# Attention stacks filled by 6 transfers of 32 rows in place of 12 transfers of 16 rows

## What is computed

```
q, k, v = heads of (normalised, modulated x) @ Wqkv + bias      # 16 heads x 16 dimensions
att     = softmax(q @ k^T * scale)                              # 512 x 512 for each head
x       = x + gate * ((att @ v) @ Wproj + bias)
x       = x + gate * (gelu(norm(x) @ W1 + b1) @ W2 + b2)        # blocks 0, 1, 2
```

## Time and profile before

| | us |
|---|---|
| median of 3 runs (lowest, highest) | 1201.08 (1197.64, 1203.54) |
| the profiled execution: its time | 1197.83 |
| its span in the profile | 1196.0 |
| TensorE matmuls busy | 1116.3 (93%) |
| TensorE weight loads busy | 713.5 (60%) |
| ScalarE busy | 806.0 (67%) |
| VectorE busy | 706.2 (59%) |
| POOL busy | 487.5 (41%) |
| DMA: bytes, mean rate | 64.49 MB, 54 GB/s |
| mean granted TensorE clock | 0.966 of full speed |

### The profile page before, as it was taken

The page is one execution under the profiler, slowest core; times in us unless marked ns, Lnnn a source line. Parts: engine busy times, 40 slices in busy tenths (PEclk is TensorE's granted clock), DMA queues, the critical chain, the costliest instruction groups (busy, mean ns, idle before and its releaser), DMA issues.

```text
span 1196.0 us, 19984 instructions
## 1 busy us (share of the span) xinstructions
PE 1116.3 (93%) x6681; PEld 713.5 (60%) x6681; DVE 706.2 (59%) x1448; ACT 806.0 (67%) x1439; POOL 487.5 (41%) x443
## 2 busy tenths in 40 slices
PE   8889999789989989999999999999999999999886
PEld 6566876654656556656556666566566466445343
DVE  7544556535264373335865855856847747888783
ACT  2563656387887688786677686687775676676563
POOL 1542642513642525453255354254353253435042
PEclk9899999899999989999999999999999999999897
DMA  7000001224414203331242232133213303342401
GB/s 227 19 26 27 1 18 22 44 52 98 87 34 82 53 15 82 65 63 20 43 89 66 57 72 45 19 77 59 56 24 54 63 1 76 55 80 44 79 14 44
DMA packets 40997, 64.49 MB, mean 54 GB/s; under 512 B 11816, under 2 KB 26920, under 8 KB 40896
## 3 DMA queue, kind: packets, MB, share of 16 engines
q1 hardware_dynamic: 40896, 63.21, 25.6%
HBM read 22.90 MB, written 2.12 MB: 21 GB/s over the span
## 4 chain that ended last, share of the span: by engine, by line
PE 64%; ACT 11%; DVE 10%; issue 8%; POOL 3%; SPq 3%; DMA 1%; ACTq 0%; POOLq 0%; DVEq 0%
PE ring L584 12%; PE ring L585 11%; PE ring L586 11%; PE AVB L694 10%; PE ring L681 8%; PE ring L658 4%; ACT probs L872 4%; DVE m L1180 3%; SPq L537 3%; PE ring L714 2%; DVE stats L1038 1%; DVE m L1164 1%; ACT L872 1%; ACT gT_h L938 1%; PE ring L627 1%
## 5 line engine op out<-in xcount | busy, mean ns | idle before, releaser
L872 ACT ACTIVATE probs<-ring 128x512 f32<-128x512 f32 x768 | 399.1, 615 | 147.2 <-PE ring L658 83.9
L1180 DVE TENSOR_REDUCE m<-ring 128x1 f32<-128x512 f32 x512 | 318.7, 682 | 126.2 <-PE ring L658 111.9
L681 PE MATMUL ring<-SQ,SK 49*128 49x512 f32 x768 | 238.0, 445 | 18.7 <-ACT probs L872 8.3
L658 PE MATMUL ring<-SK,SQ 48*128 48x512 f32 x512 | 200.0, 461 | 4.2 <-ACT probs L872 2.4
L681 PEld LDWEIGHTS ring<-SQ,SK 49*128 49x128 f32 x768 | 112.2, 189 | 153.4 <-issue 77.1
L694 PE MATMUL AVB<-probs,V 128*32 128x512 f32 x1536 | 197.1, 624 | 0.0
L1281 POOL TENSOR_TENSOR gT_l<-gT_f,gT_h 128x512 fp32r<-128x512 f32 x96 | 121.1, 1283 | 82.8 <-ACT gT_h L938 80.9
L584 PE MATMUL ring<-w_h,gT_h 128*128 128x256 f32 x384 | 110.7, 288 | 1.0 <-POOL gT_l L1281 0.7
L658 PEld LDWEIGHTS ring<-SK,SQ 48*128 48x128 f32 x512 | 86.5, 188 | 37.7 <-ACT probs L872 28.0
L585 PE MATMUL ring<-w_l,gT_h 128*128 128x256 f32 x384 | 108.0, 281 | 0.0
L586 PE MATMUL ring<-w_h,gT_l 128*128 128x256 f32 x384 | 107.8, 281 | 0.0
(11 more groups left out here) (182 smaller groups left out, 2128.7 us busy)
## 6 DMA issues: line engine op xcount, KB each, us to landing
SQ<-qh SPq DMA_DIRECT2D x192, 64.0 KB, 2.3
SK<-kh SPq DMA_DIRECT2D x192, 64.0 KB, 2.3
SQ<-ql SPq DMA_DIRECT2D x96, 64.0 KB, 2.3
SK<-kl SPq DMA_DIRECT2D x96, 64.0 KB, 2.3
raw<-in_w SPq DMA_DIRECT2D x20, 256.0 KB, 2.8
wmod_s<-in_wmod SPq DMA_DIRECT2D x6, 512.0 KB, 5.0
gates<-gate_rows SPq DMA_DIRECT2D x12, 256.0 KB, 3.6
raw<-in_wqkv SPq DMA_DIRECT2D x9, 256.0 KB, 2.8
```

The source lines that it names most:

```text
L658: mm = pe.matmul(o[:, :], SQ[a % 4][r:r + KS, n // 2, c * P:(c + 1) * P], SK[a % 4][r:r + KS, n // 2, :], start=True, stop=True)
L681: mm = pe.matmul(o[:, :], SK[a % 4][r:r + KS + 1, n // 2, c * P:(c + 1) * P], SQ[a % 4][r:r + KS + 1, n // 2, :], start=True, stop=True)
L872: act.activation(probs[:, n % PROBS, :], bank(kind, a, i)[:, :], ACT.Exp, scale=SCALE[layer(unit_job(a))]).then_inc(done["scores"], 1)
L1180: nc.vector.tensor_reduce(m16[:, 80 * (a % 2) + col:80 * (a % 2) + col + 1], bank(kind, a, i)[:, :], AX_X, ALU.max, negate=True).then_inc( ...
```

## The change

The row of dimension d, part r, of a half is now 64 * half + 4 * d + r. A part is thus the rows r, r + 4, r + 8, ... of the whole tile, and the 32 contiguous source rows of both halves fill them in one transfer of 32 partitions x 4 KB (128 KB): 6 DMAs for a unit, not 12. The order of the rows in a contraction is free, as long as SQ and SK have the same one. The rows 3, 7, ..., 63 of a half have no part. The last of them (63, KS = BLK - 1) is the shift row. The others are zero in SQ and one in SK, and add nothing. A max matmul contracts 63 rows where it had 48, a scores matmul 64 where it had 49. SQ has to be set to zero once, which four memsets on POOL do before the diagonal of ident is made. Everything else stays.

```diff
-KS = 3 * HD
+KS = BLK - 1
 ...
         def STACK_IN(u):
-            return 16 * 12 * ((u - UNITS * BATCH) // 4 + 1)
+            return 16 * 6 * ((u - UNITS * BATCH) // 4 + 1)
 ...
                     for stack, parts in ((SQ[a % 4], (qh, ql, qh)), (SK[a % 4], (kh, kh, kl))):
                         for r, part in enumerate(parts):
-                            for par in range(2):
-                                src = part[2 * HD * g + HD * par:2 * HD * g + HD * par + HD, :, :]
-                                dst = stack[BLK * par + HD * r:BLK * par + HD * r + HD, :, :]
-                                sp.dma_start(dst.bitcast(F32), src.bitcast(F32)).then_inc(stacked[a % 4], 16)
+                            src = part[2 * HD * g:2 * HD * g + 2 * HD, :, :]
+                            sp.dma_start(stack[r:P:4, :, :].bitcast(F32), src.bitcast(F32)).then_inc(stacked[a % 4], 16)
 ...
             link(nc.gpsimd.memset(ident[:, :], 0.0))
+            for i in range(4):
+                link(nc.gpsimd.memset(SQ[i][:, :, :].bitcast(F32), 0.0))
             pool.wait_ge(dve_seq, 1)
```

## The result

| | before | after |
|---|---|---|
| median, us (lowest to highest, runs) | 1199.45 (1197.64 to 1203.54, 4) | 1181.33 (1180.6 to 1182.63, 4) |
| ratio, 95% interval | | 0.9859 [0.9828, 0.9891] |
| profiled execution: time, span, mean granted clock | 1197.83, 1196.0, 0.966 | 1181.5, 1179.7, 0.979 |

The change makes the kernel 1.4% faster, 18.1 us by the medians and 16.3 us between the two profiled executions. The prediction had 5.4 us less and a range that ended at 1187. The gain is over three times the one forecast and lies outside the range.

What follows compares the result with a forecast made beforehand. The prediction took TensorE, nearly full in blocks 2 and 3, as the bound, with two shift-row waits of 4.7 us behind SP's stacks. Terms 3.65 + 1.0 + 0.25 + 0.5 = 5.4 us gave 1195.7 us, range 1187 to 1203.

Steps and rivals of the forecast that it cites:

- Matmuls: TensorE's 1280 max and scores matmuls: 63 or 64 rows take as long as 48 or 49; 0 us.
- Issue on SP: SP's stack issues halve, so shift rows go out sooner at units 55 and 59: 3.65 us less, bounds 0 to 4.7.
- The clock behind the long wait: TensorE after its 3.44 us wait at unit 59: clock may no longer fall; 1.0 us less, bounds 0 to 1.5.
- First max of a unit: TensorE's max matmul waiting for the whole stack: 0.25 us less, at unit 40 only.
- Weight loads behind a stack: ScalarE's 2.76 us idle at 659.6 us, its load queued behind unit 38's stack: 0.5 us less, bounds 0 to 2.76.
- The transfers themselves: DMA engines: same bytes, 0.73 us for a 32-row transfer against 0.36 for one of 16; the sum stays the same.
- Rival C: DMA engines: denser transfers with spread rows land later, making the kernel slower, 1205.4 us; chance 0.15.
- Start: Four POOL memsets, about 0.95 to 5.1 us, hidden in POOL's wait until 5.57: 0 us, bounds 0 to 3.8.
- Rival D: Kernel start: POOL's memsets are not covered and cost 3.8 us, giving 1199.5 us; chance 0.05.
- Sum: Whole kernel: 3.65 + 1.0 + 0.25 + 0.5 = 5.4 us less, from a median of 1201.08 to 1195.7 us.
- Rival A: SP's 30 us in the chain set the pace; halving them gives 15 us, 1186 us; chance 0.18.
- Rival B: Gain absorbed by VectorE's maxima or ScalarE's exponentials; 0 to 3 us remain, about 1199.5 us; chance 0.15.

Runs made afterwards that it cites:

- e_rows: Kernel before with its 12 transfers, but contractions of 63 and 64 rows and SQ zeroed by memsets on POOL: 1192.55 us, ratio 0.997.
- e_memset: Kernel before with only the four memsets of SQ on POOL added: 1198.69 us, ratio 1.0014.
- e_47: Kernel after, still six transfers, with contractions cut to 47 and 48 rows (last 4 of each head's 16 dimensions left out): 1188.18 us, ratio 0.9924.
- The pair at unit 60: e_35 beside a repeat of the unchanged kernel after (1183.63 us, ratio 0.9871), compared 8 us before and behind unit 60's shift transpose.
- e_split: Kernel after with each transfer cut in two: 12 transfers of 16 rows, still four apart, 63 and 64 rows contracted: 1194.95 us, ratio 0.9979.
- e_35: Kernel after, still six transfers, with contractions cut to 35 and 36 rows (7 of each head's 16 dimensions left out): 1195.26 us, ratio 0.9992.

## Why the prediction was wrong

**Matmuls.** This is the step that failed. It asked whether 15 more rows make a matmul longer, found that they don't (right: 440 and 459 ns against 445 and 461), took 0 and wrote "Below nothing: a faster one is not plausible". What the rows change is not the length of a matmul at a given clock but the clock over thousands of them. e_rows against e_memset has 18.9 us less at half clock by the rows alone, the kernel after against e_47 19.3 us less, and with the six transfers in place that is 6.0 us of time where the prediction had 0. At 0.33 us each, 19.3 us are 6.4. The row that could have raised the question stood in the text: 0.95 of full clock from 940 to 1160 us while TensorE was 94% busy. Two waits of 4.7 us could not account for it.

The two profiled executions put the clock higher than that: 83.4 - 51.2 = 32.2 us less at half clock, 10.6 us of their 16.3. The means over all executions have 22.8 us less, 7.5 of 15.1 us: the profiled execution of the kernel before had more time at half clock than most.

The Trainium skill (TensorE: Matmul & The Clock Gate, What's actually happening) says that the clock is set by how busy the array has been recently. The pair at unit 60 does not bear this out for the share of time with a matmul in flight: in the 8 us ahead that share was equal, and then the clocks were 0.57 and 1.00.

**Issue on SP.** Right in mechanism and in size at its two places: 3.6 us for 3.65, 2.69 us from copy to scores for 2.67, 0.59 us for an issue of 32 rows. Its reach was undersized. It was priced on the kernel as it stood. e_rows and e_split show that with more rows and 12 transfers the waits are 7.6 and 7.2 us, so the shorter queue is also what lets the clock's gain through. And the transfers as a whole brought 9.1 us in e_47, where the prediction's whole sum was 5.4: 3.5 us of waits, 1.1 of the weight load below and 1.2 of the clock are 5.8, and some 3 us stay unexplained.

**The clock behind the long wait.** Right where it was placed. The kernel before takes 4.24 us for eight matmuls and an av group behind the long wait; the kernel after takes 3.01 us from 1097.53 us to
```profile
1100.54 0.50 PE L680 MATMUL ring<-SQ,SK 64*128 64x512 f32 x1
```
That is 1.2 us for the 1.0 forecast. The error was to think of the clock only there.

**First max of a unit** and **Weight loads behind a stack.** 0.25 and 0.5 us. The first is too small to be told apart. For the second, TensorE's instructions after 662 us stand 1.1 us further ahead than those before it, and ScalarE's wait is gone: twice the estimate, inside its bounds. e_47 has the same lead there.

**The transfers themselves.** The sum took 0, rightly, but 0.73 us a transfer was too much. The queue's share fell from 25.6% of 1196.0 us to 20.2% of 1179.7 us, 306 to 238 us on each engine. There are 576 stack rows of 4 KB on each, so 0.12 us less for a row. The packets in the trace say the same: a packet of 4 KB took 0.38 us on average before and 0.26 after. The queue also has 4608 packets fewer (40896 and 36288), one of 4 bytes for each of the 288 transfers saved and each of the 16 engines. The Trainium skill's two figures (SBUF — State Buffer, Door 1: The DMA port swizzle), worked out per port, are 26 GB/s with 4 ports and an estimated 24 with 8, for transfers of 1 MiB, so a row would take no less time; here it takes 30% less in the larger transfer, and the measurement decides. It is the size of the transfer and not the four-apart rows: e_split, with 16 rows four apart, has 25.7%. Rival C is out by this. That 97 GB/s agreed with the skill's 104 was luck: the window's rate was set by the pace of the issues, 64 KB every 0.63 us, with the engines 0.58 busy.

**Start.** Covered, as predicted. POOL's timeline after:
```profile
0.98 3.98 POOL L1262 MEMSET SQ<- 128x1024 f32 x4
5.57 0.29 POOL L1264 TENSOR_SCALAR_AFFINE_SELECT ident<-ident 128x128 f32<-128x128 f32 x1 [0.61 <-DVE sq L958]
```
The four end at 4.96 us and the diagonal starts at 5.57 as before. VectorE's own memsets ran beside them and took 0.91 us each, as before. Rival D is out, and e_memset (1.0014) confirms it.

**Sum.** For the two profiled executions: 3.6 (waits) + 10.6 (clock) + 1.1 (weight load) = 15.3 of 16.3 us. By the means over all executions: 3.6 + 7.5 + 1.1 = 12.2 of 15.1 us, so about 3 us stay unexplained. The same sum by means gives e_rows 15.0 x 0.33 - 2.9 = 2.1 us against 3.6, e_split 11.8 x 0.33 - 2.5 = 1.4 against 2.4, e_47 5.8 against 9.1. What is missing is largest in the two kernels with six transfers. The waits and the weight load are from one profile of each. Part of the miss in absolute time is the base: 1201.08 us, a median of three, lies 3.8 us above the mean 1197.3 of 56 later executions.

**Rival A** named 1186 us, 4.7 us above the measured median and nearer than my forecast. It was right in part: halving the queue brought 9.1 us in e_47, between my 5.4 and its 15. The rest of the way to the measured time was not SP's: it came with the rows. **Rival B** would have to absorb the gain, and nothing did. The prediction's own sign of being wrong, a time below 1190 "for which these waits are too small", is the one that came.

What stays open: why rows matter to the clock at all (the runs have only how often it falls); whether rows with data count more than rows with zeros in SQ, which were enough in e_rows (e_35 and e_47 also drop rows with data); and where the remaining 3 us of the six transfers come from.

## What to carry to other kernels

Where TensorE is nearly always busy in a stage and its granted clock there is still below full (94% and 0.95 here), read the clock by stage before anything else, and ask of each edit what it does to the array's work: filling rows that cost no time brought 6.0 us here, removing the visible waits 3.6. A clock gain only reaches the end if the queues that feed TensorE keep up, so take the two apart with a two-by-two of kernels. Don't price the clock from one execution of each: here that read 10.6 us where the means have 7.5. A better clock is not a better time: judge by the time, and repeat a small win before believing it.

## What the runs showed of the hardware that was not expected

- With the same list of matmuls and the same columns, TensorE was at half clock for 93.3, 72.5 and 51.2 to 57.9 us with 35, 47 and 63 rows contracted (36, 48 and 64 in the scores). Rows of zeros in SQ were enough: 79.2 us in e_memset, 60.3 in e_rows (means of 10 executions).
- The clock fell in e_35 after 8 us that were 93% busy with no idle piece but 0.45 us beside it. In before it fell after the idle 3.44 us. Long idle time is one way to lose it and not the only one.
- An SBUF to SBUF row of 4 KB took 0.26 us on a DMA engine on average when a transfer put two rows on each, 0.38 us when it put one. The median issue on SP took 0.58 to 0.60 us in both, with single ones up to 1.95 us; landing took 2.7 us instead of 2.3.
- Executions of one program spread: the kernel before by 12.0 us in 56, e_memset by 12.1, e_rows by 14.9, e_split by 8.0 and e_35 by 9.9 us in 10 each, the kernel after by 4.3 us in 12, e_47 by 0.5 us in 4. The variants of the kernel after with more matmuls on TensorE spread by 2 to 8 us in 4 or 6.
